# A two-layer metaformer on one Trainium2 core: |scores| summed over pairs of key blocks by GpSimd, layer norm on ScalarE, and another end of the expert layers' window loop

## What is computed

```
# layer 0: retention-like attention, 8 heads of 32 channels
xf = layer_norm(x)                       # over the 256 channels, eps 1e-6
q, k, v = xf @ Wq.T, xf @ Wk.T * 32**-0.5, xf @ Wv.T
qk  = (rotate(q) @ rotate(k).T) * mask   # mask: (8 heads, 1024, 1024), fixed decay
den = clip(abs(qk).sum(keys), 1.0, 50000.0)
out = (qk / den) @ v                     # per image and head
out = (out - mean) / sqrt(var + 1e-5) * ln_g + ln_b   # over a head's 32 channels
x   = x + gelu(out) @ Wo.T
# layer 1: 3x3 convolution of x normalised and quantised to 8-bit integers, plus x
# each layer then:
t = x + experts(layer_norm(x))           # tokens x 256, 8192 tokens
# gates: graph attention over 1,048,576 edges (16 numbers a token), layer norm of
#        these, mean over 4 heads, softmax over the best 2 of 4 experts
# expert e: gelu(t @ W1[e] + b1[e]) @ W2[e] + b2[e], times the gate, summed over e
```

## Time and profile before

| | before |
|---|---|
| median of 3 runs | 5088.27 us (5087.75 to 5093.19) |
| the profiled execution's own time | 5043.97 us |
| its span in the profile | 5042.2 us |
| busy PE / PEld | 3694.2 us (73%) / 2076.2 us (41%) |
| busy DVE | 2948.2 us (58%) |
| busy ACT | 1463.4 us (29%) |
| busy POOL | 1128.7 us (22%) |
| mean granted clock of TensorE | 0.849 |
| attention, 0 to 1290 us: PE, DVE, ACT, POOL busy | 1199.9, 821.6, 642.7, 209.8 us; clock 0.99 |
| expert layer 1, 1290 to 3045 us | 1164.4, 975.1, 384.1, 449.2 us; clock 0.80 |
| convolution, 3045 to 3297 us | 165.6, 176.8, 53.1, 20.3 us; clock 0.76 |
| expert layer 2, 3297 to 5042 us | 1164.4, 974.7, 383.5, 449.4 us; clock 0.81 |

### The profile page before, as it was taken

The page is one execution under the profiler, slowest core; times in us unless marked ns, Lnnn a source line. Parts: engine busy times, 40 slices in busy tenths (PEclk is TensorE's granted clock), DMA queues, the critical chain, the costliest instruction groups (busy, mean ns, idle before and its releaser), DMA issues. The chain is left out here.

```text
span 5042.2 us, 55046 instructions
## 1 busy us (share of the span) xinstructions
PE 3694.2 (73%) x18868; PEld 2076.2 (41%) x18868; DVE 2948.2 (58%) x6308; ACT 1463.4 (29%) x2015; POOL 1128.7 (22%) x1134
## 2 busy tenths in 40 slices
PE   6999999999598567514984884869747741596687
PEld 2333333333365245303653553646425520364454
DVE  3666666667687356507870187778627640895027
ACT  2545555556252012101322321234102110132221
POOL 1111111111001631470033001000261166004200
PEclk9999999999698778756997986869868865798798
DMA  2000000000530000111111372252000011011137
GB/s 118 9 26 26 26 18 14 21 26 18 176 125 27 5 22 27 22 12 18 45 54 26 121 266 102 74 206 99 27 1 31 27 15 12 21 51 46 33 118 291
DMA packets 158027, 302.76 MB, mean 60 GB/s; under 512 B 32452, under 2 KB 116292, under 8 KB 152644
## 3 DMA queue, kind: packets, MB, share of 16 engines
q1 hardware_dynamic: 99076, 181.51, 10.1%
q10 hardware_dynamic: 25920, 94.38, 4.9%
q0 software_dynamic: 32768, 23.36, 2.7%
HBM read 183.64 MB, written 115.52 MB: 59 GB/s over the span
## 5 line engine op out<-in xcount | busy, mean ns | idle before, releaser
L1127 PE MATMUL l_pu<-l_tt,l_w 128*128 128x512 f32 x2048 | 1053.5, 641 | 477.4 <-ACT l_hid L1294 267.9
L1138 PE MATMUL l_pd<-l_w,l_hid 128*128 128x256 f32 x4096 | 990.9, 387 | 160.2 <-ACT l_hid L1294 129.4
L1138 PEld LDWEIGHTS l_pd<-l_w,l_hid 128*128 128x128 f32 x4096 | 800.2, 196 | 505.9 <-issue 311.0
L1294 ACT ACTIVATE l_hid<-l_pu,l_b 128x512 f32<-128x512 f32 x512 | 348.8, 686 | 1859.0 <-PE l_pu L1127 1310.9
L1127 PEld LDWEIGHTS l_pu<-l_tt,l_w 128*128 128x128 f32 x2048 | 412.6, 205 | 804.6 <-issue 641.1
L370 DVE TENSOR_TENSOR at_pr<-at_ps,at_decay 128x1024 f32<-128x1024 f32 x512 | 603.7, 1217 | 193.0 <-PE at_ps L491 191.8
L298 ACT ACTIVATE at_ab<-at_pr 128x1024 f32<-128x1024 f32 x512 | 537.3, 1055 | 523.4 <-DVE at_pr L370 492.4
L1493 DVE TENSOR_TENSOR l_one_lo<-l_iota,l_lo 128x4096 bf16<-128x4096 bf16 (+1 forms) x72 | 158.2, 2197 | 371.3 <-PE l_ph L1191 367.4
L1067 POOL DMA_INDIRECT l_g<-hs_rows,l_i_src x336 | 324.5, 966 | 226.4 <-DVE l_i_src L1655 124.6
L1012 POOL DMA_INDIRECT slots<-l_list,l_to x288 | 280.2, 973 | 299.1 <-DVE l_to L1610 215.1
L491 PE MATMUL at_ps<-at_qr,at_kr 32*128 32x512 f32 x2048 | 318.5, 641 | 23.7 <-DVE at_pr L370 11.8
(11 more groups left out here) (334 smaller groups left out, 4284.3 us busy)
## 6 DMA issues: line engine op xcount, KB each, us to landing
ys<-l_yst ACTq DMA_DIRECT2D x112, 512.0 KB
l_yb<-ys SPq DMA_DIRECT2D x28, 2048.0 KB, 9.8
l_tt<-tT ACTq DMA_DIRECT2D x36, 512.0 KB, 3.4
at_xt<-in_x SPq DMA_DIRECT2D x16, 1024.0 KB, 5.5
l_xt<-x SPq DMA_DIRECT2D x32, 512.0 KB, 4.1
tT<-l_xnT ACTq DMA_DIRECT2D x32, 512.0 KB, 4.4
l_xo<-x SPq DMA_DIRECT2D x28, 512.0 KB, 4.4
x<-at_xt SPq DMA_DIRECT2D x8, 1024.0 KB, 4.3
```

The lines of the kernel that those rows point to most:

```text
L1127: ins = pe.matmul(ps_u[q % 2][:, :], w1[:, e, c, P * q:P * q + P], tt[:, s, c, :], start=(c == 0), stop=(c == KK - 1))
L1138: ins = pe.matmul(out, hid[:, k % 2, c, P * r:P * r + P], w2[:, k % GE, c, :], start=False, stop=(c == MB - 1), skip_group_check=True)
L1294: act.activation(hid[:, k % 2, q, :], ps_u[q % 2][:, :], ACT.Gelu, bias=b1[:, k % GE, q:q + 1]).then_inc(s_act, 1)
```

## The change

It has three parts.

1. **Denominators by pairs of key blocks.** GpSimd adds |pr| of step 2k + 1 to that of step 2k, in place (`pair_sums`, 32 adds of 128x1024 per image), and TensorE's `denominators(k)` runs once per pair of steps, at the even steps from 4 on, so 16 times per image instead of 32. ab has six buffers instead of four: the even steps' two alternate, the odd steps have one, so ScalarE's magnitude of an odd step waits for the sum before (s_sum). The tables of steps are new. The clip and the squares go from u % 8 == 1 to u % 8 == 3, the squares are made in place in dn (pq is gone), t1 and t2 have one buffer each, for which a rotation waits until GpSimd has added the one before.
2. **Layer norm on ScalarE.** `normal` becomes ScalarE's Identity with a scale and a bias per token; for the bias VectorE computes minus the mean and GpSimd multiplies it by 1/std, behind its power. The statistics lie at steps 15 and 16 (four and four instructions) instead of 13 to 15, the moments at 17 instead of 16, normal at 19 to 21 instead of 17 to 19.
3. **End of the window loop.** TensorE adds to s_end before the last experts of its turn, and neither TensorE nor ScalarE waits for s_again any more; ScalarE doesn't signal at all, so VectorE waits for three. The exponential of the gates becomes a power of GpSimd, e to the v1, where `euler` holds 2.718...; ScalarE's direct experts follow each other without it.

The diff, cut to its core:

```diff
-PROJ_B = {0: 0, 3: 1, 11: 2, 14: 3}
-VAR_LAST = 2
-SPREAD = 5
-OUT = {7: 0, 9: 1}
+PROJ_B = {0: 0, 4: 1, 7: 2, 14: 3}
+VAR_LAST = 4
+SPREAD = 7
+OUT = {9: 0, 11: 1}
 SKIP = 10
 SKIPS = 0
-VAR = {12: 0, 23: 1, 30: 2}
-TRANS = {19: 0, 20: 1}
-PROJ_A = {21: 0, 22: 1, 24: 2, 25: 3}
-VALUES = {27: 0, 29: 1}
+VAR = {15: 0, 25: 1, 30: 2}
+TRANS = {21: 0, 22: 1}
+PROJ_A = {23: 0, 24: 1, 26: 2, 27: 3}
+VALUES = {28: 0, 29: 1}
+NPAIR = NQ // 2
...
+        def size(u, p):
+
+            return ab[:, 2 * (0, 1, 2, 1)[u % 4] + p, :, :]
...
-                    pool.tensor_tensor(pq[:, :], dn[:, :], dn[:, :], ALU.mult).then_inc(s_sqr, 1)
+                    pool.tensor_tensor(dn[:, :], dn[:, :], dn[:, :], ALU.mult).then_inc(s_sqr, 1)
                     pool.wait_ge(s_sqr, at(NGR, n))
-                    pool.tensor_tensor(pq[:, :], pq[:, :], sq[:, :], ALU.add).then_inc(s_pq, 1)
-
...
+                def pair_sums(k):
+                    for p in range(2):
+                        pool.wait_ge(s_a, at(2 * NQ, 4 * k + 3 + p))
+                        pool.tensor_tensor(size(2 * k, p), size(2 * k, p), size(2 * k + 1, p), ALU.add).then_inc(s_sum, 1)
+
+                for u in range(NQ):
+                    if main and u == 0:
+                        for i in range(2):
+                            pool.wait_ge(s_ring[slot("v", i, 1)], drained("v", i, 1))
+                        if tail:
+                            pool.wait_ge(s_av, at(NQ, 0))
+                        pool.sem_inc(s_go_p, 1)
+                        pool.tensor_copy(v[:, :, P:C], vs[:, :, :]).then_inc(s_vc, 1)
+                    if main and u - 1 in PROJ_B:
+                        rotated("pB", 1, PROJ_B[u - 1])
+                    if head and u - 1 in PROJ_A:
+                        rotated("pA", 0, PROJ_A[u - 1])
+                    if u % 8 == 3 and (main if u > 3 else tail):
+                        if u > 3:
+                            squares(u // 8 - 1)
+                        else:
+                            squares(3, back=1)
+                    if head and u == 17:
+                        pool.wait_ge(s_ve, at(1, 2))
+                        pool.tensor_tensor(rstd[:, :], ve[:, :], nhalf[:, :], ALU.pow).then_inc(s_pow, 1)
+                        pool.wait_ge(s_pow, at(1, 2))
+                        pool.tensor_tensor(shift[:, :], minus[:, :], rstd[:, :], ALU.mult).then_inc(s_rstd, 1)
+                    if main and u % 2:
+                        pair_sums(u // 2)
...
                 def magnitude(n):
                     act.wait_ge(s_ring[slot("s", n)], drained("s", n))
-                    if b > 0 or n >= 4:
-                        act.wait_ge(s_den, at(NQ, n // 2 - 1))
-                    act.activation(ab[:, n % 4, :, :], pr[:, n % 4, :, :], ACT.Abs).then_inc(s_a, 1)
+                    k = n // 4
+                    if n // 2 % 2 and (b > 0 or k > 0):
+                        act.wait_ge(s_sum, at(NQ, 2 * k - 1 + n % 2))
+                    if n // 2 % 2 == 0 and (b > 0 or k > 1):
+                        act.wait_ge(s_den, at(NPAIR, k - 1))
+                    act.activation(size(n // 2, n % 2), pr[:, n % 4, :, :], ACT.Abs).then_inc(s_a, 1)
...
+                def normal(first, n):
+                    act.wait_ge(s_rstd, at(1, 2))
+                    if tail:
+                        act.wait_ge(s_op, at(2, 0))
+                    for i in range(first, first + n):
+                        act.activation(xn[:, i, :], xt[:, i, :], ACT.Identity, bias=shift[:, i:i + 1],
+                                       scale=rstd[:, i:i + 1]).then_inc(s_xn, 1)
+
                 for u in range(NQ):
+                    if head and u in (19, 20, 21):
+                        normal(3 * (u - 19), 3 if u < 21 else 2)
...
-                def normal(first, n):
-                    dve.wait_ge(s_rstd, at(1, 2))
-                    for t in range(first, first + n):
-                        dve.tensor_scalar(xn[:, t, :], xt[:, t, :], mv[:, t, 0:1], rstd[:, t:t + 1],
-                                          ALU.subtract, ALU.mult).then_inc(s_xn, 1)
...
-                    if u % 8 == 1 and (main if u > 1 else tail):
+                    if u % 8 == 3 and (main if u > 3 else tail):
...
-                        if u in (13, 14, 15):
-                            statistics(3 * (u - 13), 3 if u < 15 else 2)
-                        if u == 16:
+                        if u in (15, 16):
+                            statistics(4 * (u - 15), 4)
+                        if u == 17:
                             variances()
-                        if u in (17, 18, 19):
-                            normal(3 * (u - 17), 3 if u < 19 else 2)
...
-                def denominators(u, back=0):
-
-                    hq, qn, kb = quad(u)
-                    if kb == 0 and (b > 0 or u > 0):
-                        pe.wait_ge(s_dn, at(NGR, u // 8))
-                    pe.wait_ge(s_a, at(2 * NQ, 2 * u + 2 - 2 * NQ * back))
+                def denominators(k, back=0):
+
+                    i = k % (NPAIR // NGR)
+                    if i == 0 and (b > 0 or k > 0):
+                        pe.wait_ge(s_dn, at(NGR, k // (NPAIR // NGR)))
+                    pe.wait_ge(s_sum, at(NQ, 2 * k + 2 - NQ * back))
                     for j in range(HPQ):
-                        ins = pe.matmul(ps_dn[KD * j:KD * j + KD, :], roots[:, :], ab[:, (2 * u + j // 2) % 4, j % 2, :],
-                                        start=(kb == 0), stop=(kb == 7), tile_position=(0, KD * j), skip_group_check=True)
+                        ins = pe.matmul(ps_dn[KD * j:KD * j + KD, :], roots[:, :], size(2 * k, j // 2)[:, j % 2, :],
+                                        start=(i == 0), stop=(i == NPAIR // NGR - 1), tile_position=(0, KD * j), skip_group_check=True)
                     ins.then_inc(s_den, 1)
...
-                    if main and u >= 2:
-                        denominators(u - 2)
-                    if tail and u < 2:
-                        denominators(NQ + u - 2, back=1)
+                    if main and u % 2 == 0 and u >= 4:
+                        denominators(u // 2 - 2)
+                    if tail and u in (0, 2):
+                        denominators(NPAIR + u // 2 - 2, back=1)
...
+            pool.wait_ge(s_dif, 1)
+            pool.tensor_tensor(v2, euler, v1, ALU.pow).then_inc(s_ex, 1)
...
                 unit_ranks(xb, n_more)
+                pe.sem_inc(s_end, 1)
                 experts(4 * LOOPED + 4 - IN_EXCHANGE, PRE_PAIRS, PRE_PAIRS + LOOPED, m)
-                pe.sem_inc(s_end, 1)
-                pe.wait_ge(s_again, m + 1)
-                pe.sem_inc(s_turn, 1)
             at[0] = 0
...
                 loop(every)
-                act.sem_inc(s_end, 1)
-                act.wait_ge(s_again, m + 1)
-                act.sem_inc(s_go, 1)
...
-            experts(4, PRE_PAIRS + LOOPED, PAIRS, LAST)
-            act.wait_ge(s_dif, 1)
-            act.activation(v2, v1, ACT.Exp).then_inc(s_ex, 1)
-            experts(4 * (PAIRS - PRE_PAIRS - LOOPED), PRE_PAIRS + LOOPED, PAIRS, LAST)
+            experts(4 * (PAIRS - PRE_PAIRS - LOOPED) + 4, PRE_PAIRS + LOOPED, PAIRS, LAST)
...
-                dve.wait_ge(s_end, m * 4 + 4)
+                dve.wait_ge(s_end, m * 3 + 3)
```

More of the change, by code:

```diff
@@ L62, in bank_pairs @@
         order += [("s", 2 * u), ("s", 2 * u + 1)]
+        if u == SPREAD:
+            order += [("bc", 0), ("bc", 1)]
         if u in PROJ_B:
@@ L151, in attention_layer @@
         s_proj, s_rot, s_vps, s_vc = (sem(k) for k in ("proj", "rot", "vps", "vc"))
-        s_sc, s_a, s_av, s_den = (sem(k) for k in ("sc", "a", "av", "den"))
+        s_sc, s_a, s_av, s_den, s_sum, s_pow = (sem(k) for k in ("sc", "a", "av", "den", "sum", "pow"))
         s_o, s_dn, s_sqr, s_pq, s_var, s_rsd, s_bc, s_g, s_op = (
@@ L266, in turn @@
-                if head:
-                    pool.wait_ge(s_ve, at(1, 2))
-                    pool.tensor_tensor(rstd[:, :], ve[:, :], nhalf[:, :], ALU.pow).then_inc(s_rstd, 1)
-                if main:
-                    squares(1)
-                if head:
-                    for i in range(3):
-                        rotated("pA", 0, i)
-                if main:
-                    squares(2)
-                if head:
-                    rotated("pA", 0, 3)
+                    pool.tensor_tensor(dn[:, :], dn[:, :], sq[:, :], ALU.add).then_inc(s_pq, 1)
@@ L559, in turn @@
                         outputs(NQ + u - 1, back=1)
-                    if main and u in PROJ_B:
-                        project("pB", 1, PROJ_B[u])
-                    if tail and u == VAR_LAST:
-                        variance(3, back=1)
                     if tail and u == SPREAD:
@@ L572, in turn @@
                             ins.then_inc(s_bc, 1)
+                    if main and u in PROJ_B:
+                        project("pB", 1, PROJ_B[u])
+                    if tail and u == VAR_LAST:
+                        variance(3, back=1)
```

50 lines of the change are left out of this document (17 added, 33 removed).

## The result

The changed kernel takes **5002.83 us** (median of 4 runs, 5000.84 to 5005.88); the kernel before 5088.01 us (4 runs, 5077.64 to 5093.19). The ratio is 0.9836, 95% interval 0.9819 to 0.9853: 85 us faster. Forecast were 4999 us in a range of 4945 to 5050.

A forecast was written before the change was run, and what follows sets the result against it. TensorE was taken to bound attention, and a hand shake at the window loop's end to hold VectorE some 103 us per expert layer. Attention -46 and loop -43 gave -89 from 5088.27: 4999 us, range 4945 to 5050.

The forecast's parts named there:

- Attention, -46: Attention loop: denominators save 14.1 us per image, waits and clock cost 8.4; net -5.7, over eight images -46.
- late sums: Attention turn: GpSimd's adds finish late for TensorE's denominators, by 0.8 us at pair 0, 2.6 at 8, 2.3 at 9.
- the walk: Step-by-step estimate of one attention turn with the adds on GpSimd: 9.9 us of lateness, net 8.4 per image.
- its worth is in the walk alone: Layer norm's last step to ScalarE: eight 0.4 us instructions leave VectorE; worth counted only within the attention turn's estimated waits.
- The row with 1423 ns: Profile row of VectorE's layer norm instruction: 402 ns, 1423 at most; read as the one that collides with GpSimd.
- The loop's end, -43: End of the window loop in both expert layers: earlier signal and gates start the tail sooner, 21.6 us each, -43.
- the rest keeps its pace: Expert layers' tails: after the second stored tile the work goes on as before, with two or three buffers full.
- the 131 us: Expert layers' tail: taking longer than 131 us from its first combination would show the forecast wrong.
- Slower by exclusion: Rival, attention: GpSimd's adds and VectorE's weighs can't run together; a turn is 204 us, total 5447; chance 0.04.
- Waits eat the attention part: Rival, attention: late adds and lower clock lose what the denominators gave; only the loop's 43 stays, 5045; chance 0.12.
- The handshake brings nothing: Rival, window loop's end: something else held VectorE 103 us; attention as forecast, total 5042; chance 0.03.
- The base of the sum: Whole kernel: -89 against the profiled execution's 5043.97, 0.9% below the median, with the difference applied to the median 5088.27.

The follow-up runs named there:

- a half alone: Kernel before with only the new attention: 4225.17 us (0.9892); with only the new end of the window loop: 4226.09 us (0.9895); kernel before there 4270.18.
- condition B: Unchosen measuring condition of some follow-up groups, under which the kernel before takes about 4270 us, against about 5085 in the result's condition.

## Why the prediction was right, point by point

- **What bounds.** Both readings held: attention is TensorE's (fewer matmuls shortened it, and its waits lengthened it again), and the 103.6 us were the hand shake, not the DMA that the row named: with the hand shake changed they are 1.09.
- **Attention, -46.** -45.4 between the traces, -45.0 as a half alone. The parts were less exact than the sum, so that it came this close is in part luck. Between the copies of v, seven turns took 46 us less together (the first 0.1, the other six 7.6 on average), against 5.7 each for eight; the first copy came 3 us later, and the stretch behind the last was 3 us shorter. Per middle turn the waits came to 14.1 - 7.6 = 6.5 us, not 8.4. The **term mis-sized** was the late sums, 0.8, 2.6 and 2.3 for pairs 0, 8 and 9 in the walk: pair 0 shows no wait on TensorE, pair 8 shows 1.97, and pair 9 shows 1.2 to 1.3 for three of eight images. With the squares behind the adds the waits for pair 9 are gone and a turn is 2 us shorter; that run moves the squares ahead of pairs 5 and 13 too, so what pair 9 alone cost isn't known. The add, taken at 2.45 us, was 2.37.
- **Layer norm, "its worth is in the walk alone".** Wrong in size: the move is worth 17 us by itself, and 47 once the adds are there. The row with 1423 ns named the cause rightly; the walk gave it no price. The 45 us of the attention half hang on this move: without it attention was longer than before the change.
- **The loop's end, -43.** -44.1 as a half alone. From TensorE's first direct group to VectorE's second stored tile it was 45.4 us and is 24.4, 21.0 less where 21.6 were forecast. The first combination follows the issue of the load of yb by 11.7 us (forecast 11, for which the prediction's 2884.3 should read 2884.05; nothing hangs on it). The gates are ready 68 us ahead, not 54. One step failed in small: "the rest keeps its pace". From the first to the last combination the tails take 133.6 and 134.6 us, before 132.0 and 130.4. That is above the 131 us which the prediction itself named as a sign of being wrong, a mark that layer 1 of the kernel before already exceeded. It costs 1.6 and 4.2 us. With the exponential on ScalarE the same stretch is 130.3 and 132.0; the cause wasn't taken apart.
- **The rivals.** "Slower by exclusion" didn't come: the weigh, with one input in PSUM, keeps its 1216 ns, while an add of the same shape with both inputs in SBUF goes from 1215 up to 2059 beside GpSimd. So the same mechanism is real for other instructions. "Waits eat the attention part" is what happens when the layer norm's step stays on VectorE. "The handshake brings nothing" fell: it brings 44.
- **The base of the sum.** It was set against a profiled execution 44 us under its median and carried over to it. That was right: the medians differ by 85 us where the two traces differ by 43. The two halves, timed alone under condition B, bear the 85 out.

## What to carry to other kernels

A wait at the end of a loop costs what stands behind it on every engine: ask for each signal whether the next thing needs it, and let TensorE give it before its long work. When work is given to GpSimd, look first at which VectorE instructions get longer beside it, and move those away: here a tensor_scalar within SBUF and an add of two SBUF inputs did, statistics with one SBUF input and products with one PSUM input didn't. One step of 0.4 us, 64 times, took back the whole gain of attention. Then look where the idle time went: here 68 us ahead of a load that could have been issued earlier were worth half of the change again.

## What had not been expected of the hardware

- The same kernel takes 5085 us under one condition and 4270 under another, with attention and conv equal: each stretch of gating is 1565 us in one and 1175 in the other. Under the first, engines other than GpSimd stand still for 5 to 34 us at a time without a releaser in the program while GpSimd issues indirect DMAs. What holds them was not tested, nor whether it belongs to the chip.
- A VectorE tensor_scalar of 128x256, 396 ns at least, takes 2520 ns at most where GpSimd adds of 128x1024 (2372 ns) run beside it, and 1124 in the median. Those that touch no add have a median of 401.
- VectorE and GpSimd hold each other up both ways. In the run with the adds on VectorE, the add, 1210 ns at least, takes up to 2059 when it starts just behind GpSimd's copy of v; and that copy, 1037 ns otherwise, takes 1224 to 2100 where it starts beside a running add of VectorE, longer by nearly what was left of that add.
